# Sampling and projecting a strip in six units instead of two halves, with the positions on VectorE

## The reference

```python
coarse_up = jax.image.resize(coarse, (B, H, W, Cc), 'bilinear')
attn = sigmoid(conv1x1(mean(fine, (1, 2)), attend_w))
fine_cal = conv1x1(fine * (attn + 1.0), select_w)
align = conv1x1(concatenate([fine_cal, coarse_up * 2.0], -1), offset_w)
om = conv3x3_same(align, om_w, om_b)
off  = om[..., :2*8*9]          # two offsets for each of 8 groups and 9 taps
mask = sigmoid(om[..., 2*8*9:])
aligned = dcn_v2(coarse_up, off, mask, dcn_w, dcn_b)
out = x + relu(aligned) + fine_cal
```

## Time and profile before

| | |
|---|---|
| runs | 3747.83, 3737.2, 3745.19 us; median 3745.19 us |
| profiled execution | 3750.21 us, its span 3748.5 us, mean granted clock 0.956 |
| TensorE (PE) | 3383.5 us busy, 90% |
| VectorE (DVE) | 2643.4 us busy, 71% |
| ScalarE (ACT) | 1636.7 us busy, 44% |
| GpSimd (POOL) | 1300.2 us busy, 35% |
| largest groups | projection L1420 1269.5 us (x8172), products L975 938.6 us (x1024), transposes L981 715.9 us (x4608), batch copies L986 651.8 us (x1152), sampling L1003 350.2 us (x16384) |

### The profile page before, as it was taken

One profiled execution on the slowest core, in us unless ns is written; L12 is line 12 of the kernel. 1 busy time (PEld: TensorE's weight loads), 2 busy tenths in 40 slices (PEclk: granted clock), 3 DMA queues, 4 the chain that ended last, 5 costly groups with the idle time before them and its releaser, 6 DMA issues.

```text
span 3748.5 us, 103646 instructions
## 1 busy us (share of the span) xinstructions
PE 3383.5 (90%) x39276; PEld 3082.7 (82%) x39276; DVE 2643.4 (71%) x4029; ACT 1636.7 (44%) x3018; POOL 1300.2 (35%) x1358
## 2 busy tenths in 40 slices
PE   8979999999999947998888998998899898988998
PEld 7869999999999936888787887887788787877888
DVE  3446666666666548878876887886887887688882
ACT  0021211211221215656654665664666665566663
POOL 1000000000000025645645555554654655455451
PEclk9989999999999978999998999998999998999998
DMA  4232232222223221111112111112111112111110
GB/s 160 78 122 42 48 72 42 48 53 39 51 51 43 32 49 30 29 32 31 31 32 32 32 33 29 31 34 32 29 33 31 30 34 36 25 33 32 31 27 23
DMA packets 352248, 159.43 MB, mean 43 GB/s; under 512 B 228724, under 2 KB 346884, under 8 KB 351620
## 3 DMA queue, kind: packets, MB, share of 16 engines
q1 hardware_dynamic: 325456, 109.56, 17.4%
q10 hardware_dynamic: 21724, 26.37, 2.1%
q0 software_dynamic: 4608, 16.78, 1.2%
HBM read 104.60 MB, written 55.23 MB: 43 GB/s over the span
## 4 chain that ended last, share of the span: by engine, by line
PE 44%; issue 7%; ACT 6%; DVE 2%; POOL 2%; ACTq 1%; DMA 1%; SPq 1%; POOLq 0%; DVEq 0%
PE eb L1420 25%; PE tb L981 9%; PE vb L1003 9%; ACT wtT L986 4%; ACT ot L1025 1%; ACT res L1012 1%; DVE wt L975 1%; PE tb L911 1%; DMA win<-cpad 1%; ACTq L1316 1%; PE vb L1018 1%; ACT val L1289 1%; ACTq L882 0%; DVE val L1362 0%; SPq L1083 0%
## 5 line engine op out<-in xcount | busy, mean ns | idle before, releaser
L1420 PE MATMUL eb<-val,wd 128*128 128x256 f32 (+2 forms) x8172 | 1269.5, 300 | 9.5 <-POOL gate L1212 8.5
L1420 PEld LDWEIGHTS eb<-val,wd 128*128 128x128 f32 x8172 | 1080.6, 199 | 44.8 <-issue 35.4
L975 DVE TENSOR_TENSOR wt<-taps_all 128x576 f32<-128x576 f32 x1024 | 938.6, 984 | 52.5 <-PE tb L981 44.6
L981 PE MATMUL tb<-ident,wt 128*128 128x128 f32 x4608 | 715.9, 282 | 63.8 <-ACT wtT L986 45.3
L986 ACT COPY wtT<-tb 128x512 f32<-128x512 f32 x1152 | 651.8, 593 | 164.8 <-PE tb L981 126.0
L1362 DVE TENSOR_TENSOR val<-vb,val 128x432 fp32r<-128x432 f32 (+1 forms) x768 | 382.6, 552 | 411.0 <-ACT val L1289 409.2
L981 PEld LDWEIGHTS tb<-ident,wt 128*128 128x128 f32 x4608 | 504.7, 141 | 185.5 <-ACT wtT L986 103.6
L1289 ACT CAST val<-vb 128x432 fp32r<-128x432 f32 (+1 forms) x768 | 342.1, 524 | 706.4 <-PE vb L1003 706.2
L480 PE MATMUL conv<-fine,wf 128*108 128x256 f32 x4608 | 591.1, 289 | 7.6 <-DVE omT L751 7.6
L480 PEld LDWEIGHTS conv<-fine,wf 128*108 128x108 f32 x4608 | 570.5, 173 | 23.0 <-issue 23.0
L1003 PE MATMUL vb<-wtT,win 64*32 64x144 f32 x16384 | 350.2, 309 | 184.3 <-issue 93.3
(11 more groups left out here) (138 smaller groups left out, 3175.7 us busy)
## 6 DMA issues: line engine op xcount, KB each, us to landing
win<-cpad SPq DMA_DIRECT2D x304, 64.0 KB
om_s<-om_d SPq DMA_DIRECT2D x1152, 12.0 KB
chunk<-in_x SPq DMA_DIRECT2D x32, 512.0 KB, 5.9
xchunk<-in_x SPq DMA_DIRECT2D x32, 512.0 KB, 4.2
r_d<-r POOLq DMA_DIRECT2D x32, 512.0 KB, 3.2
rt<-r_d SPq DMA_DIRECT2D x63, 256.0 KB, 2.9
out<-ot ACTq DMA_DIRECT2D x63, 256.0 KB, 2.2
om_d<-omT SPq DMA_DIRECT2D x64, 216.0 KB
```

Of the source, the lines that this page charges most:

```text
L975: return nc.vector.tensor_tensor(wt[:, g * NK:(g + 1) * NK, WQ * u:WQ * (u + 1)].rearrange("p k (a b) -> p k a b", a=WIN), of_group(0).uns ...
L981: last = nc.tensor.transpose(tb[b][:, 128 * j:128 * j + 128], wt[:, 4 * i + j, :], ident[:])
L1420: done = nc.tensor.matmul(eb[fo][:, W * r0:W * r1], wd[wp][:, half, k, 128 * fo:128 * fo + 128], source[:, at:at + r1 - r0, cols], start=f ...
```

## The change

- **Units.** A strip is six units: three tap rows (in the order lower, middle, upper: `ROWS = (2, 1, 0)`) times two column halves. Each unit has 12 tap-and-group slots: two products on VectorE of 768 elements, three batches of transposes, 64 sampling calls of 48 columns (3 taps x 16 pixels), one cast on ScalarE of 768 elements and two splits on VectorE of 384. `wt` and `wtT` are of the same size, now three buffers of a third (`n_sub(at) = at % 3`).
- **Order.** Each queue is a function of one unit's slot. TensorE: a batch of transposes, 5 projection products of the unit three back, sampling of the unit one back, a batch, 7 products, a batch, 6 products. ScalarE: copy, cast of the unit one back, copy, copy; behind slot 0 and 2 the taps of a half, behind slot 1 the offsets, behind 3 the relu, behind 5 the result. VectorE: first the split of the unit one back, then the products of the unit two ahead; half caps behind slots 1 to 4, the positions behind slot 5. GpSimd: side columns of the unit one back, then distances (slots 0 and 1), the gate (slot 2), the residual (slot 4).
- **Positions** and `coef` are made by VectorE (`locate`), ten steps and one.
- **The ring** `val` has 10 rows, so that every strip reads one place and no product is cut in two. Its rows 8 and 9 are copied to 0 and 1 by four DMAs of SyncE ahead of every even strip (`duplicate_rows`), in place of GpSimd's copy.
- **Banks.** `vb` is two pairs of banks, one for a unit; `eb` is one bank a strip with both output halves, into which the result is transposed as well.
- **Windows** are loaded in two parts, one for each column half.
- The loop body is still two strips; the written-out end is one pair shorter. `base_y` and `ctr_y` have 16 rows in place of 64.

```diff
@@ positions and products
-        NPOS = 8
+        NPOS = 10
...
+            for u in range(2):
+                step(0, lambda: g.tensor_tensor(posv[:, 0, u], omv[:, 0, u], by, ALU.add))
+                step(0, lambda: g.tensor_tensor(posv[:, 1, u], omv[:, 1, u], bx, ALU.add))
...
+        ROWS = (2, 1, 0)
+        PER = 3 * GH
+
+        def tap_weights_of(q, d, sub, u):
+
+            shape = [128, PER, WIN, WIN]
+            first = GK // 2 * u + PER * ROWS[d]
+            of_row = lambda t: tap[q][:, t, first:first + PER]
             return nc.vector.tensor_tensor(
...
+        def sample(sub, b, window):
+
+            for j in range(BLK):
                 for u in range(2):
-                    for g in range(GH):
+                    for c in range(GH):
                         part = slice(WQ * u, WQ * (u + 1))
-                        weights = wtT[part, g * NK:(g + 1) * NK].rearrange("p k (y x) -> p k y x", y=4)
...
+                        weights = wtT[part, PER * sub:PER * (sub + 1)].rearrange("p (k c) (y x) -> p c k y x", k=3, y=4)
+                        last = nc.tensor.matmul(values_of(b)[32 * c:32 * c + 32, u, :, :, 4 * j:4 * j + 4],
+                                                win[part, window(j), 32 * c:32 * c + 32], weights[:, c, :, :, 4 * j:4 * j + 4],
                                                 start=True, stop=True)
@@ SyncE
+                def duplicate_rows(s):
+
+                    done, read = (UNITS * s, 3 * (s - 1)) if isinstance(s, int) else (sp.to_reg(UNITS * s), sp.to_reg(3 * (s - 1)))
+                    sp.wait_ge(consts, CONSTS)
+                    w(sp, "sides", done)
+                    w(sp, "projected", read)
+                    for v in val:
+                        for half in range(CH):
+                            sp.dma_start(v[:, half, 0:6, 0:2].bitcast(f32), v[:, half, 0:6, 8:10].bitcast(f32)
+                                         ).then_inc(sems["duplicated"], 16)
@@ GpSimd
+                        t = 2 * it + p
+                        for at in range(UNITS):
+                            side(*unit(t, p, at, -1))
+                            if at == 0:
+                                measure(t + 1, 1 - p, 0)
+                            if at == 1:
+                                measure(t + 1, 1 - p, 1)
+                            if at == 2:
+                                open_strip(t, p, crossing if p == 0 else None)
+                            if at == TURN_AT:
+                                add_rest(t - 1)
@@ ScalarE
+                def slot(t, p, at):
+                    for i in range(3):
+                        if known(t, 0, ST):
+                            n = UNITS * t + at
+                            w(act, "batched", batch_no(t, at, i) + 1)
+                            w(act, "sampled", n - 2)
+                            copy_batch("act", n_sub(at), i, bank_no(t, p, at, i)).then_inc(sems["tb_out"], 1)
+                        if i == 0:
+                            keep_values(*unit(t, p, at, -1))
+                    if at == 0:
+                        taps(t + 1, 1 - p, 0)
+                    if at == OM_AT and known(t + 2, 0, ST):
+                        keep(t + 2, batch_no(t, OM_AT, 3), bank_no(t, p, OM_AT, 3))
+                    if at == 2:
+                        taps(t + 1, 1 - p, 1)
...
@@ VectorE
+                def locate(s, p):
+                    if known(s, 0, ST):
+                        h(dve, "dist_ready", 4 * s)
+                        h(dve, "masked", s + 1)
+                        positions(dve, nc.vector, s, sems["pchain"], NPOS * s)
+                        h(dve, "pchain", NPOS * (s + 1))
+                        nc.vector.tensor_tensor(coef[p][:], lo[:, 0], mask[:], ALU.mult).then_inc(sems["coef_ready"], 1)
...
+                def slot(t, p, at):
+                    split_values(*unit(t, p, at, -1))
+                    products(*unit(t, p, at, 2))
+                    if at in (1, 3):
+                        begin_cap(t + 1, 1 - p, at // 2)
+                    if at in (2, 4):
+                        end_cap(t + 1, 1 - p, at // 2 - 1)
+                    if at == 5:
+                        locate(t + 2, p)
@@ TensorE
+                AFTER = (0, 5, 12, 18)
...
+                def project_part(s, p, d, half, piece):
+
+                    if known(s, 0, ST + 1):
+                        if half == 0 and piece == 0:
+                            w(pe, "ready", s + 1)
+                            if d == 0:
+                                pe.wait_ge(wd_lo, CH)
+                                w(pe, "ob_out", s - 1)
+                            elif known(s, 0, ST):
+                                w(pe, "sides", UNITS * s + 2 * d + 2)
+                        last = project(s, p, d, range(EACH * half + AFTER[piece], EACH * half + AFTER[piece + 1]))
...
+                def slot(t, p, at):
+                    target, q, pos = unit(t, p, at, -3)
+                    for i in range(3):
+                        if known(t, 0, ST):
+                            n = UNITS * t + at
+                            if i == 0:
+                                w(pe, "products", 2 * (n + 1))
+                            w(pe, "tb_out", batch_no(t, at, i) - 1)
+                            transpose_batch(n_sub(at), i, bank_no(t, p, at, i)).then_inc(sems["batched"], 1)
+                        project_part(target, q, pos // 2, pos % 2, i)
+                        if i == 0:
+                            sample_unit(*unit(t, p, at, -1))
+                    if at == OM_AT and known(t + 2, 0, ST):
+                        offsets_turn(t + 2, batch_no(t, OM_AT, 3), bank_no(t, p, OM_AT, 3))
+                    if at == TURN_AT and known(t - 1, 0, ST + 1):
+                        m = W if isinstance(t, int) and t - 1 == ST else 256
+                        w(pe, "summed", t)
+                        turn_result(1 - p, m).then_inc(sems["turned"], 1)
```

More of the change, by code:

```diff
@@ L837, in sample_and_project @@
         tb = [bank(f"tb{i}") for i in range(2)]
-        vb = [[bank(f"vb{u}{i}") for i in range(2)] for u in range(2)]
+        vb = [ctx.enter_context(nc.psum_tensor(f"vb{i}", [128, CH, 512], f32)) for i in range(2)]
         eb = [bank(f"eb{i}") for i in range(2)]
@@ L1048, in known, with unit @@
                 return not isinstance(v, int) or least <= v < end
+            def unit(t, p, at, ahead):
+                n = at + ahead
+                more, pos = n // UNITS, n % UNITS
+                return t + more, (p + more) % 2, pos
             def loop(e, strips):
@@ L1122, in sp_fast @@
                     load_offsets(sp, s, True, sems["om_loaded"])
-                strip(0, 0, None)
-                for i in range(1, 4):
-                    strip(0, i, i)
-                with sp.Fori(1, 4) as m:
-                    for i in range(4):
-                        strip(0, 4 * m + i, i)
+                batch(0)
                 with sp.Fori(1, B - 1) as b:
@@ new lines, in dve_general @@
+                                        nc.vector.tensor_tensor(dst, values_of(d % 2)[:, u], dst, ALU.add).then_inc(sems["added"], 1)
+                                w(dve, "products", 6 * (t + 1))
+                                w(dve, "added", 6 * (t + 1))
+                    place = lambda q, half, hx: parts[q][:, half].rearrange("p (k y x) -> p k y x", k=NK, y=4)[
+                        :, :, :, 32 * hx:32 * hx + 32]
+                    for half, hx in ((half, hx) for half in range(CH) for hx in range(2)):
+                        nc.vector.tensor_copy(place(0, half, hx), sums[half][hx]).then_inc(sems["val_hi"], 1)
@@ L1585, in dve_general @@
+                    w(dve, "val_hi", 4 * (s + 1))
+                    for half, hx in ((half, hx) for half in range(CH) for hx in range(2)):
+                        nc.vector.tensor_tensor(place(1, half, hx), sums[half][hx], place(0, half, hx).bitcast(f32), ALU.subtract
                                                 ).then_inc(sems["split"], 1)
-                    w(dve, "split", 2 * (s + 1))
+                    w(dve, "split", 4 * (s + 1))
                     w(dve, "finished", 2 * (s + 1))
```

587 lines of the change are left out of this document (250 added, 337 removed).

## The result

| | before | after |
|---|---|---|
| runs, median | 3744.85 us (3737.2 to 3747.83, 4 runs) | 4223.0 us (4219.02 to 4237.42, 4 runs) |
| profiled execution | 3750.21 us, span 3748.5 | 4222.65 us, span 4221.0 |
| granted clock, mean | 0.956 | 0.938 |

The ratio is 1.129, with an interval of 1.126 to 1.132: the kernel became slower by 478 us. The forecast was 4050 us in a range of 3850 to 4280. The direction holds, and the waits that were forecast are there; the size was 173 us short.

The account below looks back on a forecast made before the run. TensorE was taken to set the pace before; afterwards, queue-order waits give 38.9 us a strip plus 1.9 for the jump, 40.8 against 35.9. Over 64 strips +314 us gives 4064, adjusted to 4050 us, range 3850 to 4280.

Parts of the forecast that it names:

- the walk: One strip followed through five in-order queues from D, VectorE's start on the previous strip's last split: 38.9 us without the jump.
- The first four moments of the walk: From D: last side copy ends 1.3 us, first distances end 4.9, slot 1's third batch starts 7.95, gate opens 17.4.
- The base: The kernel before at 35.9 us a strip, read from 16 products to a strip in the sampling stage.
- The jump: Loop's jump back every second strip: TensorE loses 3.3 and 2.2 us, values come 3.8 later, 1.9 a strip.
- Sampling: TensorE's sampling of one unit, 16 rounds: 0.85 us (0.65 to 1.95), then 0.21 to the transposes.
- the round: Eight array tiles' sampling products at 48 columns: 0.053 us from starts 6.6 ns apart, bounds 0.04 and 0.12.
- rival B: A small sampling product costs as much as a long one, round stays 0.12 us: 4250 us, chance 0.12.
- Side copy: GpSimd's side columns behind a unit's split: the walk's first runs from D+1.0 to D+1.3 us.
- The 5 us of interference: VectorE's time lost a strip beside GpSimd's four distances and its add: 5 of its 32.5 us.
- A: Rival: the walk overstates waits, VectorE's work alone sets the pace: 33.8 us a strip, 3615 us, chance 0.13.
- C: Rival: the row copy by DMA lands 8 us late in half of the strips: 4305 us, chance 0.06.
- D: Rival: the costs cancel, no change; chance 0.06 together with others.

Follow-up runs that it names:

- experiment 1: The changed kernel with GpSimd's residual add queued ahead of the side copy of unit 3 in slot 4: 4062.6 us against 4223.0.
- experiment 2: The changed kernel with positions moved to VectorE's slot 4 and half 0's distances to GpSimd's slot 5, a strip ahead: 4044.5 us against 4223.0.
- experiment 8: The changed kernel with add ahead of side copy, positions in slot 4 and half 0's distances in slot 5, side copies still on GpSimd: 3906.3 us.
- experiment 9: The changed kernel with side copies on VectorE, positions in slot 4 and half 0's distances in slot 5, a strip ahead: 3837.5 us.
- experiment 6: The changed kernel without the row copies by DMA and the waits on them: 4222.4 us against 4223.0.
- experiment 3: The changed kernel with each GpSimd side copy made as two operations of 8 elements instead of one of 16: 4302.2 us against 4223.0.
- experiment 7: The changed kernel with the side copies made by VectorE between a unit's split and its products: 3858.4 us against 4223.0.

## Why the prediction was right, and where its size came from

**Right.** Direction, range and the waits. ScalarE's taps wait for the distances in every strip, projection for the gate and the result's transposes for the add in each of 36, a batch of transposes for ScalarE in 25 cases. The first four moments of the walk hold within 0.7 us, the gate within 0.05. That is luck in part: the side copy ended 0.65 us late, and the distances behind it made that up, since the second of them had VectorE idle beside it and took 1.18 us where the walk had 1.75. Experiments 1, 2 and 8 show by removal that 317 of the 478 us hang on the order of the add, the distances and the positions.

**The sum.** Forecast +4.9 us a strip, 40.8 against 35.9. Gate intervals without a batch start alternate, by their medians, between 30.4 and 39.7 us before, 35.0 on the mean, and between 43.3 and 41.9 after, 42.6: +7.6. The 2.7 us between are 0.9 of the base and 1.8 of the walk.

- *The base.* The 35.9 us were read rightly from 2000 to 3600 us (every product is in the trace, 1024 = 64 x 16), but three batch starts lie in those 44.5 strips. The walk has none in it, so the base to hold against it was 35.0.
- *The walk without the jump* gave 38.9; the strip above has 42.0. This is the step that was mis-sized, from the gate to slot 5, and all but the last of its parts came out long:

| us | forecast | this strip | mean of even and odd strips (5th to 60th, without batch starts) |
|---|---|---|---|
| gate to split of unit 2 | 2.9 | 4.25 | 3.5 |
| split of unit 2 to split of unit 3 | 5.0 | 5.2 | 5.8 |
| split of unit 3 to end of the add | 3.1 | 3.9 | 3.9 |
| end of the add to split of unit 4 | 3.9 | 5.5 | 5.4 |
| split of unit 4 to end of positions | 6.6 | 5.8 | 6.7, with the jump |

- *The clock.* The walk took each stall as its length alone. In the 28 even strips of these the first part takes 4.3 us where a stretch at 0.50 stands behind the gate (12 of them) and 3.3 where none does; the fourth takes 5.4 with one (18 of them) and 4.0 without. So a stretch costs the engine 1.0 to 1.4 us where it stands.
- *The side copy and the add* (third part) took 0.80 and 1.97 us beside products in place of 0.3 and 1.8.
- *Waits for issue.* A stretch that is missing does not make the strip shorter. Even strips with one behind the gate last 41.7 us by median, those without 42.5: in the latter TensorE mostly stands still in the middle of sampling, between the splits of units 2 and 3 (7.3 us in place of 5.2). The walk had no such wait outside the jump. The windows of two even strips, with three and with one stretch at 0.50, and the wait in the second:

```profile
2554.46:2596.03 41.57, 35.43 (x956) 33.13 (x956) 28.08 (x44) 20.09 (x34) 13.95 (x13) 0.88 0.11 27
2639.28:2682.24 42.96, 33.78 (x956) 30.94 (x956) 28.08 (x44) 22.43 (x36) 13.94 (x13) 0.96 0.12 27
```
```profile
2646.15 1.18 PE L1012 MATMUL vb<-wtT,win 64*32 64x48 f32 x104
2648.51 0.37 PE L1012 MATMUL vb<-wtT,win 64*32 64x48 f32 x24 [1.18 <-issue]
```

- *The jump* was to cost 3.8 us every second strip. In odd strips the last part takes 7.7 us, in even ones 5.7: it costs 2.0, so 1.0 a strip in place of 1.9.

Over 64 strips 7.6 us are 486. The span grew by 473: the three batch starts together take 43 us over undisturbed intervals where they took 54, and the rest is in the start and the end. The forecast had 14 off the sum. Clock, copies and issue waits are thus read from the trace; no run took one of them away alone, and what each is worth in the period stays open.

**Terms sized otherwise.** *Sampling:* 128 products span 1.38 us and the next transposes start 1.31 us behind their first; the forecast had 0.85 + 0.21. Less the last product's length of 0.20 us, starts are 1.18 / 127 = 9.3 ns apart on the mean, not 6.6, so a round of eight is 0.07 us: nearer the lower of the bounds. The 1.38 us are more than the 1.1 that were to confirm the round, but far from the 2.2 of rival B, which is out. The Trainium skill, "TensorEngine Tiling (Array Packing)", Instruction Overhead, has some 60 cycles for each product however short; the trace disagrees for tiles side by side, 9.3 ns being 22 cycles at 2.4 GHz. *Side copy:* 0.80 us, not 0.25, since VectorE's products begin right behind the split. *Positions:* 2747.07 to 2750.18, 3.1 us, the lower bound; the walk took 3.7, which gave back 0.6 us. *VectorE's work:* 1023 / 1600 x 43.0 = 27.5 us a strip, not 32. The 5 us of interference did not come: no product takes more than 0.97 us, with or without GpSimd's distances beside it, and only cap operations are longer (2.33 for 1.35 us). The walk was near in spite of it since most of VectorE's excess lay in its idle time.

**Rivals.** A (VectorE's throughput) fell with the waits. Its condition was met in experiment 9, where ScalarE no longer waits for distances: the six units took 3837 us, not 3615. C fell by experiment 6, D by the result.

**What remains.** With both stalls gone (experiment 8) the kernel is still 159 us behind the one before. TensorE's waits in it, 2000 to 3600 us:

```profile
PE vb L1012 <- issue: 75.7, 62, 2.1
PE vb L1012 <- DMA win<-cpad: 39.5, 3, 14.2
PE tb L993 <- issue: 37.1, 23, 2.1
PE eb L1463 <- POOL gate L1231: 36.2, 21, 3.9
PE tb L993 <- DVE wt L987: 28.9, 18, 2.0
PE eb L1463 <- POOL val L1206: 16.5, 42, 0.5
PE eb L1463 <- issue: 14.1, 18, 1.0
```

and in the kernel before, beside the earlier trace rows:

```profile
PE vb L1003 <- ACT wtT L986: 37.9, 23, 1.7
PE tb L981 <- ACT wtT L986: 24.7, 44, 0.6
PE vb L1003 <- DMA win<-cpad: 11.4, 2, 6.1
...
PE eb L1420 <- POOL gate L1212: 6.5, 3, 2.3
```

The stretch holds 41.4 strips of the one and 44.5 of the other (2982 and 3204 recorded transposes, 72 a strip). TensorE is busy 32.6 us a strip in place of 32.1, and stands still 6.0 in place of 3.9: 2.7 us more in all. Waits for issue are 3.1 us a strip in place of 1.6, the gate's 0.9 in place of 0.1, those for windows 1.0 in place of 0.3, those for VectorE's products and the side copies 1.1 in place of none, while 1.6 us of waits for ScalarE's copies are gone. The windows' share may cost nothing: by the gate intervals a batch start costs 15 us in this kernel and 18 in the one before. All this is by reading; no run took one of these waits away. The sampling calls are three times as many, and the instruction queue moves 9.63 MB in 588 packets where it moved 5.91 MB in 361, which may be what the waits for issue are; this stays open.

## What to carry to other kernels

On an in-order queue, don't put an operation that waits for the newest result ahead of operations whose inputs are long there: taking six copies of 16 elements, 5 us of GpSimd's time in 43, off its queue gave back 365 of 4223 us, and reordering the queues around them 317. When a structure is cut into smaller units, walk one period with every queue, allow for a slow clock behind long stalls and for waits for issue, and compare the walk with a period that, like it, holds no batch start. Work put on the engine that "has time" cost, for 3.1 us of positions, 1.9 us a strip in one structure and 0.7 in the other, and 3.4 us more ahead of the last split cost 3.1: it goes by what is queued behind.

## What the runs showed of the hardware

- A GpSimd copy of 16 elements takes 0.80 us beside VectorE's two-input products; where VectorE was idle the copy of 24 elements in the kernel before took 0.23; one of 8 elements takes 0.85 beside them (experiment 3). VectorE's products beside it are at most 0.97 us. The Trainium skill, "SBUF — State Buffer", SBUF: two separate sides, says that VectorE with two inputs and GpSimd lock the shared ports for a whole instruction and that the later one waits; the copy at 2709.31 us, begun 0.21 us into a product of 0.95 us and ended 0.07 us behind it, agrees. The next product, begun at 2709.96 while the copy still ran, took 0.96 and had not waited.
- Which of the two is held up changes with their order: with the side copies off GpSimd (experiment 7) 45 of 506 products, all beside GpSimd's operations, took over 1.2 us and up to 2.00; in the changed kernel none of 436 did, and GpSimd's distances were long instead.
- A distance of GpSimd beside VectorE's products takes 1.89 us, with VectorE idle 1.18 (both in the strip above).
- Stalls of TensorE of about the same length were followed by a granted clock of 0.50 for 3.4 us or by none: in the strip above after 2.23 and 2.29 us, but not after 2.25. Between 2000 and 3600 us, of the 36 stalls ahead of the result's transposes (2.2 to 2.3 us each) 24 had such a stretch begin within about 1.5 us of their end.
